# Four-layer graph attention kernel: last results of layer 0 ahead of layer 1's edges, earlier maxima at the end of layer 1, flag and bias split moved

## What is computed

```python
# layer 0: row softmax
h = x @ W.T ; e = leaky(s1[:, None] + s2[None, :])
out = softmax(where(adj == 0, -1e9, e), axis=-1) @ h
# layer 1: column softmax, then elu
out = elu(softmax(where(adj > 0, e, -9e15), axis=1) @ h)
# layer 2: like layer 0 with a bias in h and in s1, s2, then elu
Wh = x @ W.T + b ; s1 = Wh @ ai + bi ; s2 = Wh @ aj + bj
# layer 3: four relations, one weight each
y = sum_r ((adj == r) @ x) @ weight[r] + bias
```

## Time and profile before

| | |
|---|---|
| median of 3 runs | 470.44 us (469.98 to 471.45) |
| profiled execution | 470.86 us, its span 469.1 us |
| busy share of the span | PE 81%, DVE 80%, ACT 67%, POOL 62% |
| mean granted TensorE clock | 0.93 |

### The profile page before, as it was taken

The page is one execution under the profiler, slowest core; times in us unless marked ns, Lnnn a source line. Parts: engine busy times, 40 slices in busy tenths (PEclk is TensorE's granted clock), DMA queues, the critical chain, the costliest instruction groups (busy, mean ns, idle before and its releaser), DMA issues. The chain is left out here.

```text
span 469.1 us, 9311 instructions
## 1 busy us (share of the span) xinstructions
PE 378.9 (81%) x2818; PEld 337.8 (72%) x2825; DVE 375.9 (80%) x1414; ACT 315.8 (67%) x805; POOL 290.5 (62%) x425
## 2 busy tenths in 40 slices
PE   2789998998666779778697787899999959888870
PEld 2689998997666779678696676899999855455440
DVE  0167999999866899999999855598889997888862
ACT  1467999999534475565555655487778747787864
POOL 3236888887443545354453565478787886878882
PEclk9799999999777999899998899799999999999985
DMA  5998662000000000000000000000000000011122
GB/s 156 222 249 223 121 132 47 2 1 1 2 1 2 0 0 2 1 1 2 0 2 0 2 2 1 1 1 1 1 1 2 3 0 1 21 65 52 67 76 86
DMA packets 8757, 18.21 MB, mean 39 GB/s; under 512 B 1280, under 2 KB 2560, under 8 KB 8704
## 3 DMA queue, kind: packets, MB, share of 16 engines
q0 software_dynamic: 2304, 8.39, 9.4%
q1 hardware_dynamic: 2976, 4.52, 2.9%
q10 hardware_dynamic: 3424, 4.66, 2.8%
HBM read 21.76 MB, written 4.19 MB: 55 GB/s over the span
## 5 line engine op out<-in xcount | busy, mean ns | idle before, releaser
L461 PE MATMUL o_ps<-h_scaled,PT 128*128 128x129 f32 (+1 forms) x1536 | 193.8, 288 | 17.1 <-DVE y L953 14.2
L461 PEld LDWEIGHTS o_ps<-h_scaled,PT 128*128 128x128 f32 x1536 | 188.8, 204 | 18.5 <-issue 14.9
L669 ACT ACTIVATE X<-y,offset,rstd 128x128 f32<-128x128 f32 x256 | 104.9, 482 | 38.9 <-POOL offset L270 38.7
L901 DVE SCALAR_TENSOR_TENSOR PT<-rows_ps,factors,MT 128x512 f32<-128x512 f32 x128 | 88.8, 737 | 0.8 <-PE rows_ps L448 0.6
L403 PE MATMUL h_ps<-wx,xT 128*128 128x130 f32 x384 | 66.7, 314 | 27.9 <-DVE smax L856 26.9
L403 PEld LDWEIGHTS h_ps<-wx,xT 128*128 128x128 f32 x384 | 56.5, 211 | 38.3 <-issue 37.2
L261 POOL TENSOR_TENSOR rstd<-var_eps,neg_half 128x4 f32<-128x4 f32 x64 | 66.4, 1038 | 5.0
L973 DVE BATCH_NORM_STATS2 stats<-y 128x6 f32<-128x128 f32 x256 | 56.0, 281 | 7.0 <-DVE y L967 0.5
L276 POOL TENSOR_TENSOR elu_exp<-elu_exp,X 128x512 f32<-128x512 f32 x32 | 40.7, 1272 | 18.8 <-ACT elu_exp L663 18.5
L251 POOL TENSOR_TENSOR h_scaled<-hx,factors 128x516 f32<-128x516 f32 x32 | 33.6, 1050 | 24.7 <-PE o_ps L461 14.8
L227 POOL TENSOR_TENSOR mean_term<-h_mean,empty_row 128x512 f32<-128x512 f32 x32 | 38.2, 1192 | 16.9 <-DVE residual L953 15.3
(11 more groups left out here) (98 smaller groups left out, 664.6 us busy)
## 6 DMA issues: line engine op xcount, KB each, us to landing
MT<-adj_by_j POOLq DMA_DIRECT2D x16, 512.0 KB, 8.7
X<-x SPq DMA_DIRECT2D x16, 256.0 KB, 6.0
out<-X ACTq DMA_DIRECT2D x16, 256.0 KB, 2.0
w_rel<-w SPq DMA_DIRECT2D x1, 256.0 KB, 3.1
w_back<-w_by_output ACTq DMA_DIRECT2D x1, 192.0 KB, 3.1
wx<-w_by_input ACTq DMA_DIRECT2D x1, 192.0 KB, 5.9
bias<-b ACTq DMA_DIRECT2D x1, 64.0 KB, 4.5
bias<-b SPq DMA_DIRECT2D x1, 64.0 KB, 8.4
```

The costliest lines, as they stand in the source:

```text
L461: last = pe.matmul(o_ps[it.b][:, ic, first:1 + D], PT[:, it.b, jc, ic * P:(ic + 1) * P], h_scaled[:, it.b, jc, first:1 + D], start=(jc == ...
L669: last = act.activation(X[:, g, c, :], y[:, b, c, :], ACT.Identity, bias=offset[:, b, c:c + 1], scale=rstd[:, b, c:c + 1])
L901: dve.scalar_tensor_tensor(out=PT[:, it.b, c, :], in0=rows_ps[:], scalar=factors[:, it.b, 1, c:c + 1], in1=m, op0=ALU.max, op1=ALU.mult, * ...
```

## The change

On DVE, `take_out(at(-2))` of layer 0 moves in front of the edges and node terms (slots 14 to 17; its four instructions and their waits are the same). The maxima of items 32 and 33 are taken late in slots 29 and 30 instead of early in slots 30 and 31. The three DVE operations of the flag move to the relation layer, to slots 54, 57 and 58, and PE's transpose to slot 56, into another PSUM region (`smax_ps`); PE's slot 18 has the common order. The bias split leaves DVE's slot 8: five instructions go to POOL at the end of slot 24, three copies to ACT at the end of slot 26, with a new tile `bias2_low` for the third part.

```diff
+FLAG_SLOT = G * LAYERS + 6
+        bias2_low = sb("bias2_low", [P, 130], BF16)
 # POOL
+            def split_bias2():
+                pool.wait_ge(sem("b2_a"), 1)
+                pool.wait_ge(sem("b_in"), B_IN)
+                pool.tensor_tensor(bias2[:, D:D + 2], b2_a[:, :], ab2_sb[:, :], ALU.add).then_inc(sem("bias2"), 1)
+                pool.wait_ge(sem("bias2"), 1)
+                pool.tensor_copy(bias2_hi[:, :], bias2[:, :]).then_inc(sem("bias2"), 1)
+                pool.wait_ge(sem("bias2"), 2)
+                pool.tensor_tensor(bias2_rest[:, :], bias2[:, :], bias2_hi[:, :], ALU.subtract)\
+                    .then_inc(sem("bias2"), 1)
+                pool.wait_ge(sem("bias2"), 3)
+                pool.tensor_copy(bias2_mid[:, :], bias2_rest[:, :]).then_inc(sem("bias2"), 1)
+                pool.wait_ge(sem("bias2"), 4)
+                pool.tensor_tensor(bias2_low[:, :], bias2_rest[:, :], bias2_mid[:, :], ALU.subtract)\
+                    .then_inc(sem("bias2"), 1)
             def attention_slot(at, n):
 ...
                 if at(1) and at(1).l == 1:
                     scale_h(at(1))
+                if n == G + 8:
+                    split_bias2()
 # PE, attention_slot
-                if at(4) and n != G + 2:
+                if at(4):
                     next_transpose(at(4))
 ...
-                if n == G + 2:
-                    pe.wait_ge(sem("flag_own"), 1)
-                    pe.wait_ge(sem("xT"), at(3).done)
-                    pe.transpose(xT_ps[:, 0:P], flag_own[:, 0:1].broadcast_to([P, P]), ident[:])\
-                        .then_inc(sem("flag_ps"), 1)
-                    pe.wait_ge(sem("flag_max"), 1)
-                    next_transpose(at(4))
 # PE, relation_slot
+                if n == FLAG_SLOT + 2:
+                    pe.wait_ge(sem("flag_own"), 1)
+                    pe.transpose(smax_ps, flag_own[:, 0:1].broadcast_to([P, P]), ident[:])\
+                        .then_inc(sem("flag_ps"), 1)
 # ACT, attention_slot
                 if at(2) and at(2).l == 1:
                     column_hinge(at(2))
+                if n == G + 10:
+                    act.wait_ge(sem("bias2"), 5)
+                    act.copy(bias2_parts[0:1, :], bias2_hi[0:1, :])
+                    act.copy(bias2_parts[32:33, :], bias2_mid[32:33, :])
+                    act.copy(bias2_parts[64:65, :], bias2_low[64:65, :]).then_inc(sem("bias2_parts"), 1)
 # DVE, attention_slot
-                if n == 8:
-                    split_bias2()
                 if at(-1) and at(-1).l in (0, 2):
                     row_sums(at(-1))
-                if at(2) and not (at(2).l == 1 and at(0).l == 1):
+                if at(2) and not (at(0) and at(0).l == 1):
                     take_max(at(2))
                 if at(-1) and at(-1).l in (0, 2):
                     row_factors(at(-1))
+                if at(-2) and at(-2).l == 0:
+                    take_out(at(-2))
                 if at(1) and at(1).l == 1:
                     edges(at(1))
                 if at(2) and at(2).l == 1:
                     node_terms(at(2))
                 if at(3) and at(1) and at(1).l == 1:
                     own_max(at(3))
-                if at(-2) and at(-2).l == 0:
-                    take_out(at(-2))
 ...
-                if at(3) and at(3).l == 1 and at(1).l == 1:
+                if at(3) and at(1) and at(1).l == 1:
                     take_max(at(3))
 ...
-                if n == G + 1:
...
 # DVE, end of relation_slot
+                if n == FLAG_SLOT:
+                    dve.wait_ge(sem("flag_sum"), G)
+                    dve.tensor_reduce(flag_own[:, 0:1], flag_sum[:, :, 0], AX.X, ALU.max).then_inc(sem("flag_own"), 1)
+                if n == FLAG_SLOT + 3:
+                    dve.wait_ge(sem("flag_ps"), 1)
+                    dve.tensor_reduce(flag_own[:, 1:2], smax_ps, AX.X, ALU.max).then_inc(sem("flag_max"), 1)
+                if n == FLAG_SLOT + 4:
+                    dve.wait_ge(sem("flag_max"), 1)
+                    dve.tensor_scalar(flag_int[:, :], flag_own[:, 1:2], 0.25 * C * N, None, ALU.is_gt)\
+                        .then_inc(sem("flag"), 1)
```

More of the change, by code:

```diff
@@ L829, in _ @@
             dve.memset(hx[:, :, :, 0:1], 1.0).then_inc(sem("ones"), 1)
-            def split_bias2():
-                dve.wait_ge(sem("b2_a"), 1)
-                dve.tensor_tensor(bias2[:, D:D + 2], b2_a[:, :], ab2_sb[:, :], ALU.add).then_inc(sem("bias2"), 1)
-                dve.wait_ge(sem("bias2"), 1)
-                dve.tensor_copy(bias2_hi[:, :], bias2[:, :]).then_inc(sem("bias2"), 1)
-                dve.wait_ge(sem("bias2"), 2)
-                dve.tensor_copy(bias2_parts[0:1, :], bias2_hi[0:1, :])
-                dve.tensor_tensor(bias2_rest[:, :], bias2[:, :], bias2_hi[:, :], ALU.subtract)\
-                    .then_inc(sem("bias2"), 1)
-                dve.wait_ge(sem("bias2"), 3)
-                dve.tensor_copy(bias2_mid[:, :], bias2_rest[:, :]).then_inc(sem("bias2"), 1)
-                dve.wait_ge(sem("bias2"), 4)
-                dve.tensor_copy(bias2_parts[32:33, :], bias2_mid[32:33, :])
-                dve.tensor_tensor(bias2_parts[64:65, :], bias2_rest[64:65, :], bias2_mid[64:65, :], ALU.subtract)\
-                    .then_inc(sem("bias2_parts"), 1)
             def own_max(it):
@@ L1036, in attention_slot @@
                     aggregate(at(-1))
-                if n == G + 1:
-                    dve.wait_ge(sem("flag_sum"), G)
-                    dve.tensor_reduce(flag_own[:, 0:1], flag_sum[:, :, 0], AX.X, ALU.max).then_inc(sem("flag_own"), 1)
-                    dve.wait_ge(sem("flag_ps"), 1)
-                    dve.tensor_reduce(flag_own[:, 1:2], xT_ps[:, 0:P], AX.X, ALU.max).then_inc(sem("flag_max"), 1)
-                    dve.wait_ge(sem("flag_max"), 1)
-                    dve.tensor_scalar(flag_int[:, :], flag_own[:, 1:2], 0.25 * C * N, None, ALU.is_gt)\
-                        .then_inc(sem("flag"), 1)
             def relation_slot(at, n):
```

## The result

| | before | after |
|---|---|---|
| first measurement: median | 470.94 us (469.98 to 472.2, 4 runs) | 453.17 us (452.58 to 454.31, 4 runs) |
| ratio | | 0.9624, 95% interval 0.9591 to 0.9657 |
| second measurement: median | 469.41 us (468.23 to 471.27, 11 runs) | 454.37 us (451.78 to 458.35, 6 runs) |
| ratio | | 0.9687, 0.9644 to 0.973 |
| profiled execution, its span | 470.86 us, 469.1 us | 452.63 us, 450.8 us |

The change gains 17.8 us by the first measurement and 14.7 us by the second. The two intervals overlap only between 0.9644 and 0.9657.

A forecast was written before the change was run, and what follows sets the result against it. Between layer 0 (PE full) and layer 1's body (DVE full), DVE and PE wait for each other in turn; 3.9 + 4.1 + 2.6 + 0.1 + 1.0 - 0.1 + 1.3 - 0.3 + 1.4 = 14.0 us gives 456.4, range 454.5 to 461.0.

The forecast's parts named there:

- y ahead of the edges, slots 15 to 17: Layer 0's y right behind the reciprocal ends the mutual waits of DVE and PE: 3.9 + 4.1 + 2.6 us gained.
- PE idling elsewhere: Sign of a wrong forecast: in slots 15 to 17 PE's waits for y gone, but PE idle at other places there.
- removing the wait keeps the clock up: Answer to the rival that TensorE stays at half clock in slots 16, 17 and the next (6.7 us lost, 463.1, chance 0.05).
- Slot 14: y ahead of the node terms: PE's gain is mostly slack, 0.1 us gained, between 0.3 lost and 1.5 gained.
- Flag out of slot 17: Three small DVE operations and a wait for PE, 0.97 us before the edges, all come back: 1.0 us gained.
- Flag in the relation layer: The three operations in three different slots, two of them before idle DVE: 0.1 us lost, between 0 and 0.97.
- Split off DVE: Slot 8: maxima 7.29 us apart return to 5.95, on the path because PE never catches up: 1.3 us gained.
- GpSimd's split: Slot 24: five instructions take 2.3 us, less slack of 0.68 and 1.35, so DVE loses 0.3 us (0 to 3.3).
- The rival of a slow split: Slot 24: five GpSimd instructions at 1.05 us each take 5.3, DVE loses 3.3 instead of 0.3: 459.4 us, chance 0.08.
- a late y: Slots 15 to 17: y's inputs not ready at its new place, half of 10.6 us lost: 461.7 us, chance 0.05.
- Maxima of items 32 and 33: Layer 2's entry: maximum some 2.0 us earlier, DVE's idle 1.40 for hx goes: 1.4 us gained, between 0 and 2.0.
- the sum is made against it, and the saving carried over to the median: Savings reckoned on the profiled execution (470.86 us, 0.42 above the median), then taken off the median of 470.44.

The follow-up runs named there:

- split_early: The changed kernel with GpSimd's five bias instructions ahead of h_scaled in slot 24 instead of behind it: 455.13 us, ratio 0.9675 to the kernel before.
- bias_only: The kernel before with only the bias split moved from DVE to GpSimd and ScalarE: 468.69 us, ratio interval 0.9949 to 1.0005.
- warm_before: The kernel before with PE's idle time at the start filled by extra transposes, results unchanged: 468.65 us, ratio 0.9962.
- warm_after: The changed kernel with PE's idle time at the start filled by extra transposes: 454.21 us, ratio 0.9652 to the kernel before.
- the filled pair: The kernel before and the changed one, both with PE's idle time at the start filled by extra transposes: 468.65 and 454.21 us.
- y_flag: The kernel before with only y moved in slots 14 to 17 and the flag moved: 455.41 us, ratio 0.9694.

## Why the prediction was right and where it was wrong

The mechanism was right, and nearly all of the gain is where I put it. Step by step:

- *y ahead of the edges, slots 15 to 17:* 10.6 forecast, 11.4 shown, alike in ten of the eleven profiles that have it (10.3 in `split_early`). The waits named were 10.6. From item 17 to 20 DVE's idle fell by 10.7 and its busy time from 26.12 to 25.42, so 0.7 lay in instructions that got shorter. Against other executions of the old order, which were up to 0.8 us quicker here than before's first profile, it is 10.7 to 11.3. DVE ends last, as said, and PE idles almost only for DVE, so what I had called a sign of being wrong, PE idling elsewhere, came as mere slack. That removing the wait keeps the clock up did not hold: it still fell to 0.50 twice, and the matmuls of slots 16 and 17 stayed slow (4.77 and 5.44). The margin that I had reckoned for them held; in `split_early` it didn't, where the slot from item 18 to 19 took 9.47 us at a granted clock of 0.64 instead of 8.75 at 0.80.
- *Slot 14:* 0.1 forecast, 1.2 shown. This is the mis-sized term of the change itself. I took the lower part of my own bounds (+0.3 to -1.5) because DVE had no idle there; the time lay in a busy instruction that was long for waiting.
- *Flag out of slot 17:* 1.0 forecast, 0.7 shown, as a hinge wait of 0.31 took its place. Alone it is worth 1.2 up to item 31, after y 3.0 (14.0 - 11.0), of which 1.2 is the clock's fall behind the flag. My sum held it constant.
- *Flag in the relation layer:* 0.1 forecast; 0.37 at item 46, which I had not seen as a place of cost at all, and 0.2 at item 57, beside a y that still waits 0.9 in every second slot.
- *Split off DVE:* 1.3 forecast, 0.94 shown, since ScalarE and not PE was next. With item 48 and 61 it gains some 0.4 to 0.7 more at the end.
- *GpSimd's split:* 0.3 forecast, 0.5 lost. The instructions were quicker than assumed (1.9 against 2.3), their neighbours slower. The rival of a slow split (over 3 us) didn't occur, nor did a late y.
- *Maxima of items 32 and 33:* 1.4 forecast. In the first profile the own maximum of slot 30 comes without idle, as said, and the stretch gains 2.7.

The own maximum after (answers to the earlier trace rows):

```profile
241.47 0.26 DVE L861 TENSOR_REDUCE smax<-h_ps 128x1 f32<-128x128 f32 x1
...
246.30 0.15 DVE L856 TENSOR_REDUCE smax_own<-hx 128x1 f32<-128x4 f32 x1
```

Over the 18 profiles, items 31 to 37 gain 0.04 to 2.9 in the eight with the maxima moved, 2.2 on average, and 0 to 2.2 in the ten without, 1.05 on average. The difference is 1.1, with values this scattered good to about 1 us; that agrees with the 1.4. Before's first profile was an execution without luck there. Seven of the eight gain 1.5 by item 34, of the ten none more than 0.63; the rest comes behind, and there it is the clock's. The slot from item 36 to 37 takes 6.5 us in the three profiles in which the granted clock is 1.00 throughout (`bias_only`, `warm_before`, `warm_after`), 7.82 at 0.80 after, and 8.65 at 0.72 in before's first profile.

What failed is the step ahead of the sum: "the sum is made against it, and the saving carried over to the median". Executions of the same code differ by up to 4.3 us at the start and by about 2 us at layer 2's entry, both with TensorE's clock, and my range had nothing for it on the low side. The term that I mis-sized beside it is y ahead of the node terms: I put it at 0.1 on the ground that DVE had no idle time there, and it measured 1.2.

Without the start, and with the maxima at their mean, the terms are 0.93 + 1.21 + 11.4 + 0.69 - 0.44 + 1.1 = 14.9 us up to item 37, and 14.5 to 14.7 to the end of the span (-0.41 to -0.15). That is 0.5 to 0.7 more than forecast, and agrees with the second measurement (14.7) and the filled pair (14.4). The first one's 17.8 rests on four executions of either kernel. That it has luck in it is argued from the other two and not shown, and I can't say how much: its interval begins at 16.2 us (0.0343 x 470.94), the second's reaches to 16.7.

Open stays what decides the clock's course at the entry of layer 2; no kernel was made for it.

## What to carry to other kernels

Read the duration of each small instruction against its duration elsewhere: one that takes 1.08 us here and 0.22 there is a wait in disguise, and laying GpSimd's timeline beside DVE's shows what for. When a stall is taken away, name the engine whose own slot is next longest, by the distance of its repeated instruction (6.08 against 5.95 here): it may have lived on that stall. Before a sum is made against one execution, see which stretches of it repeat in another. And let the ledger end where the execution ends: 0.35 us that DVE gained at the last item was lost again in the last transfer.

## What the runs showed of the hardware that I had not expected

- A DVE tensor_scalar of 128 x 4 on SBUF took 0.65 and 1.08 us beside GpSimd's full-width tensor_tensor, ending with it, and 0.22 otherwise; scalar_tensor_tensor weights took 0.92 instead of 0.74, and GpSimd's 128 x 4 took 0.55 instead of 0.20, when the two fell together.
- The granted clock is 1.00 in the rows of the first 16 us, yet the projection at 12 us takes 1.94 us, as at 0.50, in every unfilled execution read; in `y_flag` the rows say 1.00 up to 34 us, beside projections of 1.94 us at 23.36 and 2.07 at 17.45. There the duration tells the clock, not the row.
- In all seven profiles with the bias split off DVE's stream (seven instructions in slot 8) idle time charged to issue is 0.3 us less some 350 us later, and in none of the eleven others.
- The last output transfer took 3.58 to 3.67 us from its issue to the end of the span when it followed the one before by 3.3 us, and 3.81 to 4.87 when it followed by 3.0.
